# Reloading five batches of transposed rows later, batch by batch, and running the router's matmuls in other slots

## What is computed

```
x = x + tanh(g_xattn) * attention(layernorm(x), ctx)   # 32 query heads, 8 key heads, window 64, alibi, two key sets
xt = layernorm(x)
probs = softmax(xt @ w_router)                         # 128 experts, the best 4 are kept
shared = silu(xt @ shared_w_gate) * (xt @ shared_w_up) @ shared_w_down
x = x + tanh(g_ffn) * (experts(xt, probs) + shared)
```

## Time and profile before

| | |
|---|---|
| time, median of 3 runs | 881.89 us (881.84 to 884.01) |
| the profiled execution's own time | 881.89 us |
| its span, from first to last instruction | 878.5 us |
| PE busy | 863.9 us, 98% of the span |
| DVE, ACT, POOL busy | 541.2, 403.7, 509.6 us |

### The profile page before, as it was taken

How to read it: one execution, slowest core, us unless ns; L and a number is a source line. 1 busy time by engine, 2 the same in 40 slices (tenths; PEclk the granted TensorE clock), 3 DMA queues, 4 the chain that set the end, 5 groups by cost and what they waited for, 6 DMA issues and landing times.

```text
span 878.5 us, 17386 instructions
## 1 busy us (share of the span) xinstructions
PE 863.9 (98%) x6662; PEld 753.6 (86%) x6662; DVE 541.2 (62%) x983; ACT 403.7 (46%) x812; POOL 509.6 (58%) x526
## 2 busy tenths in 40 slices
PE   9899999999999999999999999999999999999998
PEld 8889999999999998887878867888888888888886
DVE  7675666666766666643436848455665565565567
ACT  6655555455545454655134242444444444444431
POOL 3761433435344323251599983547888888788641
PEclk9999999999999999999999999999999999999999
DMA  8678675767767679820102244411212011111046
GB/s 274 169 153 178 151 206 172 205 190 180 201 164 209 162 191 278 164 82 18 49 25 63 94 133 158 156 31 67 72 42 80 25 72 51 46 73 48 1 145 238
DMA packets 77947, 110.17 MB, mean 125 GB/s; under 512 B 7329, under 2 KB 49058, under 8 KB 76834
## 3 DMA queue, kind: packets, MB, share of 16 engines
q1 hardware_dynamic: 75656, 108.04, 43.9%
q10 hardware_dynamic: 2210, 1.03, 0.5%
HBM read 71.76 MB, written 32.05 MB: 118 GB/s over the span
## 4 chain that ended last, share of the span: by engine, by line
PE 87%; DMA 4%; POOL 3%; DVE 2%; issue 2%; SPq 1%; ACT 1%; POOLq 0%; DVEq 0%
PE ps_scores L2199 20%; PE ps_proj L1822 15%; PE ps_scoresT L2199 10%; PE ps_scoresT L1959 7%; PE ps_o L1973 6%; PE ps_proj L1811 5%; PE ps_scores L1932 5%; PE ps_proj L2199 5%; PE ps_proj L1880 4%; PE ps_scores L1822 4%; PE ps_scoresT L1822 3%; DMA q_stack<-max_rows 1%; DMA k_kept<-kT_lo 1%; DMA ctx_turned<-in_ctx 1%; DMA xn_rows<-in_x 1%
## 5 line engine op out<-in xcount | busy, mean ns | idle before, releaser
L1110 ACT ACTIVATE probsT<-ps_scoresT 128x512 f32<-128x512 f32 (+1 forms) x256 | 138.8, 545 | 150.1 <-PE ps_scoresT L1959 145.7
L1461 DVE TENSOR_REDUCE neg_max<-ps_scores 128x2 f32<-128x384 f32 (+1 forms) x256 | 131.8, 517 | 109.2 <-PE ps_scores L1932 108.4
L1328 ACT ACTIVATE part_sums<-ps_scores 128x512 f32<-128x512 f32 x96 | 57.5, 599 | 134.8 <-PE ps_scores L2199 130.4
L1959 PE MATMUL ps_scoresT<-q_stack,k_stack 116*128 116x256 f32 x448 | 106.0, 307 | 0.3 <-DMA q_stack<-max_rows 0.3
L827 POOL TENSOR_TENSOR o_normal<-o_blocks,inv_sums 128x256 f32<-128x256 f32 x32 | 19.9, 622 | 141.8 <-DVE inv_sums L1482 141.8
L1932 PE MATMUL ps_scores<-k_stack,q_stack 114*128 114x192 f32 (+1 forms) x512 | 94.5, 267 | 2.8 <-DMA q_stack<-qT_hi 1.7
L1932 PEld LDWEIGHTS ps_scores<-k_stack,q_stack 114*128 114x128 f32 x512 | 83.1, 190 | 9.5 <-DMA q_stack<-qT_hi 2.3
L973 POOL TENSOR_TENSOR w_expert_lo<-w_sums,w_expert_hi 128x256 fp32r<-128x256 f32 x64 | 63.9, 1009 | 45.4 <-ACT w_expert_hi L1251 45.4
L985 POOL TENSOR_TENSOR big<-big,basis 128x512 f32<-128x512 f32 x56 | 77.4, 1401 | 14.9 <-DVE basis L1761 14.9
L1959 PEld LDWEIGHTS ps_scoresT<-q_stack,k_stack 116*128 116x128 f32 x448 | 70.7, 190 | 4.1 <-DMA q_stack<-max_rows 0.4
L1752 DVE TENSOR_TENSOR basis<-part_sums,silu_gate 128x512 f32<-128x512 f32 x32 | 24.2, 755 | 67.2 <-ACT silu_gate L1336 67.2
(11 more groups left out here) (311 smaller groups left out, 2496.8 us busy)
## 6 DMA issues: line engine op xcount, KB each, us to landing
k_stack<-k_kept SPq DMA_DIRECT2D x64, 192.0 KB, 4.5
big<-coeff_rows SPq DMA_DIRECT2D x8, 1024.0 KB, 4.7
q_stack<-q_kept SPq DMA_DIRECT2D x40, 192.0 KB, 4.2
q_kept<-qT_hi SPq DMA_DIRECT2D x10, 512.0 KB
x_rows<-in_x SPq DMA_DIRECT2D x9, 512.0 KB, 6.1
k_kept<-kT_hi SPq DMA_DIRECT2D x16, 256.0 KB
x_kept<-x_rows SPq DMA_DIRECT2D x16, 256.0 KB, 2.7
w_raw<-in_L_ffn_w_gate SPq DMA_DIRECT2D x16, 256.0 KB, 2.9
```

The lines of the kernel that those rows point to most:

```text
L1110: act.activation(PT[:, g % 2, 2 * j:2 * j + blocks].rearrange("p h f r w -> p (h f r w)"), ST[:, n % 2, 0:blocks].rearrange("p h n -> p (h ...
L1328: act.activation(TP[:, u % 2, j, :], src[:, u % 2, :], ACT.Copy).then_inc(taken, 1)
L1461: dve.tensor_reduce(NM[:, g // 2 % 2, g % 2, 2 * i:2 * i + 2], SA[:, n % 2, :, 0:keys], AX.X, ALU.max, negate=True).then_inc(max_done, 1)
L1959: ins = pe.matmul(ST[:, n % 2, v, :], KS[0:ROWS, g, j + v, 1 - v].rearrange("p w s -> p (w s)"), QS[0:ROWS, g, j + v].rearrange("p f r w - ...
```

## The change

Two tables change, and two waits are put otherwise.

```
-XT_AT = {-13: (0, 0), -12: (1, 0), -11: (2, 0), -9: (0, 1), -8: (1, 1), -5: (2, 1), -4: (3, 0), -1: (3, 1), 3: (4, 0), 5: (4, 1)}
+XT_AT = {-13: (0, 0), -11: (1, 0), -9: (0, 1), -6: (1, 1), -4: (2, 0), -1: (2, 1), 2: (3, 0), 4: (3, 1), 7: (4, 0), 10: (4, 1)}
...
-ROUTER_AT = {s: divmod(i, ROUTER_PIECES) for i, s in enumerate((0, 3, 4, 5, 6, 7, 9, 11, 12, 13, 14, 15, 16, 17, 19, 20, 21, 22))}
+ROUTER_AT = {s: divmod(i, ROUTER_PIECES) for i, s in enumerate((1, 3, 4, 5, 6, 7, 8, 9, 11, 12, 13, 14, 15, 16, 17, 19, 20, 21))}
...
             if part == 0:
                 if q == 0:
                     pe.wait_ge(w_lo, 2)
-                if q < TB:
-                    pe.wait_ge(pj_done, passed("wo", B - 3, q))
+                    pe.wait_ge(pj_done, passed("wo", B - 3, TB - 1))
...
-                if q < TB:
-                    pe.wait_ge(pj_done, passed("wo", B - 2, q))
+                if q == 0:
+                    pe.wait_ge(pj_done, passed("wo", B - 2, TB - 1))
```

## The result

| | before | after |
|---|---|---|
| median of 22 runs each | 882.80 us | 887.66 us |
| lowest to highest | 879.18 to 888.68 | 884.76 to 891.63 |
| ratio, 95% interval | | 1.0051 (1.0038 to 1.0064) |
| the profiled execution's own time | 881.89 us | 887.48 us |
| its span | 878.5 us | 885.3 us |

The changed kernel is slower by 0.5%: some 4.5 us by the ratio, 4.9 us from median to median, and 5.6 us from one profiled execution to the other. The page of the profile, against the earlier trace rows: PE is busy 1.8 us longer, with the same 6662 matmuls.

What follows compares the result with a forecast made beforehand. PE, busy 863.9 of 878.5 us, was taken to bound the kernel, so the change could only move waits. Terms +0.1 + 1.4 + 1.8 - 0.3 = +3.0 on 881.9 gave 884.9 us, range 881.5 to 888.5.

Steps and rivals of the forecast that it cites:

- the first wait: Slot 8: PE asks for batch 3 at 353.0, its last reload lands at 354.4; +1.4 us (0.4 to 2.0).
- The second wait: Slot 15: PE waits for batch 4's lo reload, queued behind a group and the row load; +1.8 us (0.4 to 3.3).
- The router's pieces without DMAs: Moved pieces in slots 0, 8 and 21 shift waits for DVE and ACT; together +0.1 us (-0.6 to +0.5).
- both come 2 x 1.4 = 2.8 us earlier: Batch 3's last two reloads, now seventh and eighth, land 2.8 us earlier if engines stay full, the second at 355.0.
- 4.8 if the 9.2 us stay: Upper case for slot 8's wait: batch 3's last reload still takes 9.2 us to land, a wait of 4.8 us.
- nearly independent: Slot 15's wait hangs on SP's release and hardly on slot 8's wait, so +1.4 and +1.8 us were added.
- The wait for the maxima: Slot 18: PE's wait for the DMA of the maxima is absorbed because PE comes later; -0.3 us.
- The signs named beforehand: L1822 pieces in slots 8 (0.4 to 2 us) and 15 wait for the reload DMA; DMA share under 1, 330-350 us.
- The mark set for wrong sizes: Predicted sizes are wrong if the DMA share stays at 1 and the waits pass 3 us.
- the reloads land in time: Rival: no reload waits in slots 8 and 15; 882.2 us, no change; chance 0.17.
- only small waits: Rival: waits in slots 8 and 15 both at low bounds, or one alone, 0.4 to 2.0 us; 883.2 us; chance 0.20.
- The stragglers stay: Rival: the 9.2 and 9.6 us landings stay, +4.8 and +5.3 us; 891.8, or about 888.5 with one; chance 0.12.

Runs made afterwards that it cites:

- experiment 1: Changed kernel with the kernel before's table of reloads, so only the router's slots are new; 883.36 us, ratio 1.0000.
- experiment 2: Kernel before with the change's new table of reloads, the router's slots left old; 886.80 us, ratio 1.0045.
- experiment 6: Kernel of experiment 5 with ten unread matmuls on PE ahead of the wait for batch 3 in slot 8; 885.34 us, ratio 1.0012.
- experiment 8b: Changed kernel with the next rows' load six slots later, slot 16; 888.92 us over 6 runs, ratio 1.0071.
- experiment 5: Changed kernel with batch 4's lo reload in slot 8 instead of 10, ahead of the group and row load; 886.90 us, ratio 1.0040.
- experiment 4: Changed kernel with 16 unread matmuls on PE ahead of the wait for batch 3 in slot 8; 888.83 us, ratio 1.0044.
- experiment 3: Changed kernel with batches 0 to 3 reloaded in the kernel before's slots, only batch 4 late (slots 7 and 10); 887.63 us, ratio 1.0052.
- experiment 8c: Kernel before with the next rows' load six slots later, slot 16 instead of 10, in all batches; 883.08 us, ratio 0.9989.
- experiment 7: Kernel of experiment 3 with ten unread matmuls on PE ahead of the wait for batch 4 in slot 15; 886.23 us, ratio 1.0040.
- experiment 8a: Kernel of experiment 3 with the next rows' load six slots later, slot 16; 883.85 us, ratio 0.9997.
- 9: Kernel of experiment 3 with batch 4's lo reload in slot 8 instead of 10, ahead of group and row load; 882.06 us, ratio 0.9979.
- experiment 10: Kernel before with the router's pieces in new slots, slot 8 gaining one and slot 22 losing one, slot 0 kept, reloads old; 882.43 us, ratio 0.9990.

## Why the prediction was right, and where its sum was not

The forecast was 884.9 us, within 881.5 to 888.5, with slower the likelier side. It came out slower, 887.66 us, with the mechanism that was named: reloads that land after PE asks. Yet the sum of +3.0 us is 1.5 to 2.6 us short, and its two large terms are both off. That the measured time lies within the range is in part luck: in the stretch the first wait was 2.8 us longer than its term, the second 1.3 us shorter, 2.65 us had no term at all, and outside the stretch the changed execution was 2.1 us shorter, for which no term stood either.

- **The router's pieces without DMAs, +0.1.** Experiment 1 has the same order and a ratio of 1.0000, and its profile puts the order at 0.4 us: within the bounds (-0.6 to +0.5), above the middle. Step by step: slot 1's wait for DVE became 0.48 us from 0.21 (0.47 more was expected, 0.27 came); slot 9's wait is gone. In slot 24 PE waits 0.65 us where about 0.5 was said for ACT's copy, but the one it waits for is now POOL's `oT_lo`: the copy comes early enough, and another engine stood right behind it.
- **The first wait, +1.4: it measured 4.2.** The step that failed is "both come 2 x 1.4 = 2.8 us earlier". The first of the pair did come earlier, by 0.6 us, but the second landed at 357.5 against 357.8 before, 8.7 us after its issue. The bound "4.8 if the 9.2 us stay" was what happened. Six traces have this pair at this place, and the second, issued between 348.8 and 350.7, landed at 353.7 (experiment 2), 354.7 (6), 355.7 (8b), 356.1 (5), 356.7 (4) and 357.5 us (the changed kernel). The predicted 354.4 is near the early end of that, and no single number would have been right. The DMA share from 340 to 350 us goes along with it: 0.88 and 0.92 where the landing took 4.7 us (experiments 6 and 2), 0.93 and 0.95 for 5.4 and 7.1 (5 and 4), 1.04 and 1.06 for 6.9 and 8.7 (8b and the changed kernel), at nearly the same 266 to 283 GB/s. So the engines were longer busy with as many bytes. Why in one execution and not in another is open. The Trainium skill says on "DMA: Bandwidth & Descriptors", section "Why a DMA increments its semaphore by 16 and not by 1", that only when all of the up to 16 engines have finished their share has a transfer landed. That fits a landing that scatters while the share of all engines is full, but no view here shows which engine was last.
- **The second wait, +1.8: it measured 0.46.** The prediction called the two "nearly independent". That is the step that failed. Its own landing was well sized: from the release of SP (358.95, the transposed scores of slot 9) the reload landed after 10.3 us, and 9.7 were predicted. But PE took 9.9 us over the way from there to slot 15, not 7.9, since the low clock made that way 2.0 us longer. Where the first wait was absent, the second was 2.9 and 3.2 us (experiments 3 and 2), and where the clock was kept, 1.85 (experiment 4): the predicted size. The two waits share one loss: the first, with the low clock behind it, makes the second small.
- **What the sum had no term for, +2.65.** PE's clock behind a standstill. The prediction read that it was 1.00 throughout and left it there, as if it were a constant of the kernel. Experiments 5 and 6 show the cause: PE held for as long, once standing and once at work, takes 1.67 us more when it stood. The Trainium skill warns of it on "TensorE: Matmul & The Clock Gate", section "Loop structure matters more than you think", with "long DMA wait between every matmul → PE goes cold". One wait was enough here, as the 4.21 us ahead of a stretch at 0.58 show.
- **The wait for the maxima, -0.3: absorbed.** Right in the changed kernel. That it can be 1.64 us (experiment 1) or 2.4 in two pieces (experiment 8c) was not foreseen.
- **The signs named beforehand.** L1822 in slots 8 and 15 names the DMA of the reload: so it is. The DMA share below 1: 0.84 from 330 to 340 us, but 1.06 from 340 to 350. The mark set for wrong sizes, a share that stays at 1 and waits past 3 us, was met in that half and by the first wait.

Of the rivals, "the reloads land in time" and "only small waits" are out: of the eight kernels with batch 4's last reload behind the row load or batch 3 in slots 2 and 4 (the changed one, experiments 2 to 7 and 8b) seven have a standstill of 1.85 us or more in their traces; in the eighth, experiment 6, the reload came some 0.8 us after PE was free for it, under the fill. "The stragglers stay" was half true: one of the two was kept, at +4.2 us, and the clock behind it was in no rival. The Trainium skill's estimate of 3.2 us for 512 KB in the prediction ("DMA: Bandwidth & Descriptors", section "Anatomy of one DMA") is not borne out here: the page gives its figures for transfers issued from GpSimd, while these are issued from SP, with others under way, and from 330 us on they took 5.1 to 8.7 us in the changed kernel.

Open are two things: what makes the second of the pair scatter, and why the changed execution is 0.91 and 1.2 us shorter elsewhere.

## What to carry to other kernels

When a transfer is moved towards its deadline, price its landing by the slowest one in a like place of the queue, and not by the queue's average; what stands ahead of it in the issuing engine's order has its price too (experiments 3 and 8a: the row load alone, 1.6 us of landing; experiments 3 and 9: two slots, a group and the row load, 5.3 us of the stretch). Where TensorE at full clock would stand about as long as in the executions here that lost it (1.69 to 4.21 us), read in a trace what the next microseconds cost at the lower clock, and add that to the wait: 1.6 to 3.0 us here. And do not add up two late transfers as independent waits: whatever delays PE at the first is slack for the second. Here neither the first removed alone (experiment 3, 1.0052) nor the second removed alone (experiment 5, 1.0040) gave a gain that the times can tell from the changed kernel's 1.0051.

## What the runs showed of the hardware

- **The clock's bill.** It came in two sizes. The granted clock was at its lower level for 3 to 4 us, and the same matmuls took longer by 1.59 (wait 1.85, experiment 4), 1.64 (2.17, experiment 5), 1.59 (3.05, experiment 7) and 1.60 us (3.16, experiment 2); or it was there for 6 to 7 us, and they took longer by 2.90 (2.49, experiment 8b), 2.99 (2.87, experiment 3) and 2.65 us (4.21, the changed kernel, where part of the time passed in the wait itself). So the price follows how long the clock stays down, and that does not follow the length of the wait.
- **When it falls.** After standstills of 1.24 (experiment 8a), 1.64 (experiment 1) and 1.80 us (experiment 8c) the clock stayed at 1.00; after 1.69 (experiment 10, in an earlier batch) and 1.85 us (experiment 4) it fell. Between these the length alone does not decide, and no run here shows what does.
- **The fill.** Matmuls that nobody reads, put ahead of the wait, kept the clock at 1.00 in both executions where they outlasted it (experiments 4, 6).
- **It is not one profile's accident.** Of 55 runs of the changed kernel 2 have a mean clock of at least 0.999; of experiment 3 none of 12; of experiments 1 and 9, whose profiles show no wait for a reload, 9 and 10 of 12. Of 99 runs of the kernel before beside the experiments 59 have it, with a median of 882.1 us, and the other 40 have 886.1 (22 of them, at a mean clock of 0.998, have 885.5, and 14, at 0.996, have 888.5). So the kernel before, too, seems to lose its clock at times, in a wait that its one profile does not show. Experiment 10, which has its reloads, shows one such place: the standstill at 90.68 us.
- **A reload of 512 KB** took 3.2 (experiment 6) to 12.1 us (experiment 8c) to land, in kernels that all move the same bytes.
